# Recurrent stage of a two-layer network: unrolled, and its three engines' operations put in a new order

## The reference, cut to what matters

```python
x = layernorm(x, ln0_w, ln0_b)
for l in range(L):                                   # L = 4
    h = layernorm(x, ln1_w[l], ln1_b[l])
    hh = time_shift(h)                               # the token before
    xk = h * tmk[l] + hh * (1 - tmk[l])              # xv, xr alike
    k = jnp.einsum('btc,oc->bto', xk, Wk[l])         # v alike
    sr = jax.nn.sigmoid(jnp.einsum('btc,oc->bto', xr, Wr[l]))
    rwkv = sr * wkv(time_decay[l], time_first[l], k, v)
    x = x + jnp.einsum('bto,co->btc', rwkv, Wo[l])
    h = layernorm(x, ln2_w[l], ln2_b[l])
    hh = time_shift(h)                               # xk, xr from h, hh
    kf = jnp.square(jax.nn.relu(jnp.einsum('btc,fc->btf', xk, Wck[l])))
    kv = jnp.einsum('btf,cf->btc', kf, Wcv[l])
    x = x + jax.nn.sigmoid(jnp.einsum('btc,oc->bto', xr, Wcr[l])) * kv
```

## Time and profile before

| | us |
|---|---|
| median of 3 runs | 1193.19 (1193.03 to 1208.87) |
| the profiled execution | 1198.58, span 1196.7 |
| recurrent stage in it | 728.0 to 1115.2 |
| busy in the span: TensorE, VectorE, ScalarE | 1063.7, 767.2, 578.4 |

### The profile page before, as it was taken

One profiled execution on the slowest core, in us unless ns is written; L12 is line 12 of the kernel. 1 busy time (PEld: TensorE's weight loads), 2 busy tenths in 40 slices (PEclk: granted clock), 3 DMA queues, 4 the chain that ended last, 5 costly groups with the idle time before them and its releaser, 6 DMA issues. The chain is left out here.

```text
span 1196.7 us, 13244 instructions
## 1 busy us (share of the span) xinstructions
PE 1063.7 (89%) x4046; PEld 463.8 (39%) x4046; DVE 767.2 (64%) x1327; ACT 578.4 (48%) x904; POOL 12.1 (1%) x26
## 2 busy tenths in 40 slices
PE   6788999999779999999999996498898898898698
PEld 3333444444334444444444432133333333343332
DVE  5867788887556555555555554676776776776465
ACT  5224566667644222222222224666666666767332
POOL 1000000000000000000000000000000000000000
PEclk9768999999989999999999999799899899899899
DMA  3721022200141545555555520000000000000100
GB/s 116 207 60 41 11 50 50 51 24 10 30 90 40 123 91 117 125 122 113 114 108 125 125 45 28 0 21 9 1 20 9 0 20 0 0 0 1 27 9 26
DMA packets 49975, 64.62 MB, mean 54 GB/s; under 512 B 17570, under 2 KB 41232, under 8 KB 45328
## 3 DMA queue, kind: packets, MB, share of 16 engines
q1 hardware_dynamic: 49100, 63.28, 22.5%
q10 hardware_dynamic: 832, 0.79, 0.2%
HBM read 55.87 MB, written 5.77 MB: 52 GB/s over the span
## 5 line engine op out<-in xcount | busy, mean ns | idle before, releaser
L1098 DVE TENSOR_REDUCE part_max<-psum 128x1 f32<-128x512 f32 (+3 forms) x304 | 188.1, 659 | 54.0 <-PE psum L709 31.6
L945 ACT ACTIVATE pt<-psum 128x1024 f32<-128x1024 f32 (+1 forms) x192 | 151.1, 813 | 141.1 <-PE psum L729 104.0
L1257 DVE TENSOR_TENSOR moe_gu<-moe_silu,psum 128x512 f32<-128x512 f32 x132 | 90.8, 688 | 152.0 <-PE psum L861 147.2
L1082 ACT ACTIVATE moe_silu<-psum 128x512 f32<-128x512 f32 x112 | 66.9, 597 | 200.0 <-PE psum L856 200.0
L856 PE MATMUL psum<-h,moe_wt 128*128 128x512 f32 x264 | 135.6, 595 | 1.6 <-ACT moe_silu L1050 1.6
L861 PE MATMUL psum<-h,moe_wt 128*128 128x512 f32 x264 | 135.2, 593 | 0.5 <-DVE moe_gu L1257 0.5
L866 PE MATMUL psum<-moe_hid,moe_wt 128*128 128x512 f32 x264 | 135.0, 593 | 0.7 <-DVE moe_hid L1265 0.7
L705 PE MATMUL psum<-ka,qa 72*128 72x512 bf16 (+3 forms) x384 | 121.8, 360 | 5.5 <-DMA ka<-rows_k 3.5
L726 PE MATMUL psum<-qa,ka 75*128 75x512 bf16 (+3 forms) x384 | 107.8, 344 | 7.1 <-DMA qa<-neg_t 6.8
L1265 DVE TENSOR_TENSOR moe_hid<-moe_gu,qa 128x512 f32<-128x512 f32 x120 | 83.1, 693 | 13.6 <-DVE moe_gu L1257 5.7
L1542 PE MATMUL psum<-kf,wt_c 128*128 128x512 f32 x128 | 67.8, 656 | 24.2 <-ACT kf L1671 24.2
(11 more groups left out here) (251 smaller groups left out, 1394.7 us busy)
## 6 DMA issues: line engine op xcount, KB each, us to landing
qa<-comb_rows SPq DMA_DIRECT2D x56, 512.0 KB, 6.2
qa<-rows_q SPq DMA_DIRECT2D x21, 192.0 KB
ka<-rows_k SPq DMA_DIRECT2D x21, 192.0 KB
o_den<-acc SPq DMA_DIRECT2D x32, 64.0 KB, 2.2
moe_raw<-in_L_ffn_eg_w SPq DMA_DIRECT2D x32, 64.0 KB, 5.6
moe_raw<-in_L_ffn_eu_w SPq DMA_DIRECT2D x32, 64.0 KB, 5.4
moe_raw<-in_L_ffn_ed_w SPq DMA_DIRECT2D x32, 64.0 KB, 5.1
qa<-comb_rows SPq DMA_DIRECT2D x16, 128.0 KB, 3.1
```

The costliest lines, as they stand in the source:

```text
L945: act.activation(pt[:, u % 4, :, 0:n], score_bank[u % 2][:, :, 0:n], ACT.Exp, scale=SCALE)\
L1082: act.activation(sg[:, c % 2, :], g_bank[:, :], ACT.Silu).then_inc(silu_done, 1)
L1098: dve.tensor_reduce(part_max[:, h0:h0 + heads, slot], bank_of("fill", f)[:, 0:heads * nk].rearrange("p (h n) -> p h n", h=heads), AX_X, AL ...
L1257: dve.tensor_tensor(gu[:, at % 2, :], sg[:, at % 2, :], u_bank[:, :], ALU.mult).then_inc(gu_done, 1)
```

## The change

All loops over units are unrolled in Python, so each instruction has constant operands and waits. The per-sublayer copies of parameters (`vectors_a`, `vectors_c`, L1727 to L1737) go, and the parameters are read in place. Each helper now issues the work of one chunk, and each engine has a `body(u)` for u = 1 to 8 that lists the single operations. With p = u - 1, it holds the time norm and the keys, values and receptance of u, and the output, the channel norm and the channel products of p. The products `gated` of a unit and the product with the gates, `finish` and `residual` stand at the start of the next body on VectorE. On ScalarE `log_den` and `inverse` stand there too, so the sigmoid is no longer ahead of them. The time weights have two buffers. The weights' transposes are spread over the body. The last body does in place of a time norm the norm of the first two chunks for the final stage. At the stage's start the sigmoid of unit 0 stands ahead of the inverse, and `gate_time` and `finish` behind the entry norm of batch 1.

```diff
+def here(u, q):
+    return hp[:, u % 2, 1 + q * CH:1 + (q + 1) * CH]
+def before(u, q):
+    return hp[:, u % 2, q * CH:(q + 1) * CH]
+def vec(v, u):
+    return G.vec[:, 4 * v + u // 2:4 * v + u // 2 + 1]
-def layers(eng, body):
-    with eng.Fori(0, LAYERS - 1) as l:
-        body(l, 0)
-        body(l, 1)
-    body(LAYERS - 1, 0)
-    body(LAYERS - 1, 1, last=True)
+    return n0 + 4 * u + 8 + q
-    with sp.Fori(0, LAYERS - 1) as l:
+    for l in range(LAYERS - 1):
-def turn_c(l, u):
+def turn_c(l, i):
+    if i < 2 and l:
+        pe.wait_ge(relu_done, 8 * (2 * l - 1) + 7 + i)
+    if i < 2 and not l:
+        pe.wait_ge(v_kept, 1 + i)
+    if i == 2:
+        pe.wait_ge(r_mid, 2 * (2 * l) + 2)
     pe.wait_ge(c_in, 48 * (l + 1))
-    for i in range(9):
-        if i == 8:
-            pe.wait_ge(r_mid, 2 * u + 2)
-        mm = pe.transpose(G.bank[(6, 7, 5)[i // 4]][:, chunk(i % 4, P)], raw_c[:, i, :], G.ident[:, :])
-        if i % 4 == 3 or i == 8:
-            mm.then_inc(c_turned, 1)
...
-def body(l, b, last=False):
-    u = 2 * l + b
-    for q in range(2):
-        pe.wait_ge(r_new, 2 * u + q + 1)
-        if not last:
-            ln_centre(pe, G, ln_time(u + 1, q), G.r[:, seq(1 - b, q)], q)
-        output(u, q)
-        if not last:
-            ln_variance(pe, G, ln_time(u + 1, q), q)
-    if not last:
-        if b == 0:
-            turn_c(l, u)
-        else:
-            turn_a(l + 1)
-    norm(lambda q: ln_channel(u, q), b, lambda q: pe.wait_ge(r_mid, 2 * u + q + 1))
-    if last:
-        for c in range(2):
-            pe.wait_ge(G.x_l1, c + 1)
-            ln_centre(pe, G, G.ln_count + c, G.x[:, chunk(c)])
-        for c in range(2):
-            ln_variance(pe, G, G.ln_count + c)
-    if not last:
-        if b == 0:
-            pe.wait_ge(c_kept, 3 * (l + 1))
-        else:
-            pe.wait_ge(a_kept, l + 2)
-        kvr(u + 1, 1 - b)
-    channel_mix(u, last)
...
+def time_centre(u, q):
+    if u == UNITS:
+        pe.wait_ge(G.x_l1, q + 1)
+        ln_centre(pe, G, ln_time(u, q), G.x[:, chunk(q)], q)
+    else:
+        if u:
+            pe.wait_ge(r_new, 2 * u - 1 + q)
+        ln_centre(pe, G, ln_time(u, q), G.r[:, seq(u % 2, q)], q)
+def keys(u, q):
+    if u == UNITS:
+        return
+    pe.wait_ge(h_time, 2 * u + q + 1)
+    if q == 0:
+        pe.wait_ge(a_kept, u // 2 + 1)
+    if q == 1 and u % 2:
+        pe.wait_ge(c_kept[2], u // 2 + 1)
+    shifted(G.bank[4 + q], u, K_HERE, K_BEFORE, q).then_inc(k_psum, 1)
+def values(u, q):
+    if u == UNITS:
+        return
+    if u % 2:
+        pe.wait_ge(c_kept[q], u // 2 + 1)
+    shifted(G.bank[6 + q], u, V_HERE, V_BEFORE, q).then_inc(v_psum, 1)
+def receptance(u, q):
+    if u == UNITS:
+        return
+    if u:
+        pe.wait_ge(G.ln.scaled, ln_channel(u - 1, q) + 1)
+        shifted(G.bank[q], u, R_HERE, R_BEFORE, q).then_inc(r_psum, 1)
+    else:
+        pe.wait_ge(k_kept, q + 1)
+        shifted(G.bank[4 + q], u, R_HERE, R_BEFORE, q).then_inc(r_psum, 1)
 def output(u, q):
-    pe.wait_ge(wd, STEPS * u + 17 + q)
-    pe.matmul(G.bank[4 + q][:, :], wt_a[:, WO, :], rw[:, chunk(q)], start=True, stop=True).then_inc(o_psum, 1)
...
+def up(u, q, j):
+    n = 4 * q + j
+    if n == 0:
+        pe.wait_ge(c_kept[0], u // 2 + 1)
+    if n < 2 and u < LAST:
+        pe.wait_ge(v_kept, 2 * (u + 1) + n + 1)
+    else:
+        pe.wait_ge(relu_done, 8 * u + n - 1)
+    if j == 0:
+        pe.wait_ge(mixed_k, 2 * u + q + 1)
+    pe.matmul(G.bank[6 + j % 2][:, :], wt_c[:, WCK + j, :], mix_c[:, 0, q, :], start=True, stop=True)\
+        .then_inc(f_psum, 1)
+def down(u, q, j):
+    pe.wait_ge(kf_done, 8 * u + 4 * q + j + 1)
+    if j == 0 and u < LAST:
+        pe.wait_ge(k_kept, 2 * (u + 1) + q + 1)
+    if j == 0 and u == LAST:
+        pe.wait_ge(r_mid, 2 * u + q + 1)
+    if q == 0 and j == 0:
+        pe.wait_ge(c_kept[1], u // 2 + 1)
+    mm = pe.matmul(G.bank[4 + q][:, :], wt_c[:, WCV + j, :], kf[:, j, q, :], start=(j == 0), stop=(j == 3),
+                   skip_group_check=True)
+    if j == 3:
+        mm.then_inc(kv_psum, 1)
+def gate(u, q):
+    if q == 0:
+        pe.wait_ge(c_kept[2], u // 2 + 1)
+    pe.wait_ge(mixed_r, 2 * u + q + 1)
+    pe.wait_ge(G.ln.rstd, ln_channel(u, q) + 1)
+    pe.matmul(G.bank[2 + q][:, :], wt_c[:, WCR, :], mix_c[:, 1, q, :], start=True, stop=True)\
+        .then_inc(cr_psum, 1)
+def body(u):
+    p, l = u - 1, u // 2
+    time_centre(u, 0)
+    if u % 2:
+        turn_c(l, 1)
+    time_variance(u, 0)
+    time_centre(u, 1)
+    output(p, 0)
+    time_variance(u, 1)
+    output(p, 1)
+    channel_centre(p, 0)
+    if u % 2:
+        turn_c(l, 0)
+    channel_variance(p, 0)
+    channel_centre(p, 1)
+    keys(u, 0)
+    if u % 2:
+        turn_c(l, 2)
+    channel_variance(p, 1)
+    keys(u, 1)
+    values(u, 0)
+    values(u, 1)
+    up(p, 0, 0)
+    up(p, 0, 1)
+    up(p, 0, 2)
+    receptance(u, 0)
+    up(p, 0, 3)
+    up(p, 1, 0)
+    down(p, 0, 0)
+    up(p, 1, 1)
+    up(p, 1, 2)
+    gate(p, 0)
+    up(p, 1, 3)
+    receptance(u, 1)
+    gate(p, 1)
+    down(p, 0, 1)
+    down(p, 1, 0)
+    down(p, 0, 2)
+    if u % 2 and u < LAST:
+        turn_a(l + 1)
+    down(p, 1, 1)
+    down(p, 0, 3)
+    down(p, 1, 2)
+    down(p, 1, 3)
...
+def keep_a(l):
+    act.wait_ge(a_turned, l + 1)
+    wt = wt_a[l % 2]
+    for i in range(3):
+        turned = G.bank[6][:, chunk(i, P)]
+        act.activation(wt[:, 2 * i, :], turned, ACT.Copy, scale=vec(TMK + i, 2 * l))
+        act.activation(wt[:, 2 * i + 1, :], turned, ACT.Copy, scale=rest[:, 4 * i + l:4 * i + l + 1])
+    act.copy(wt[:, WO, :], G.bank[6][:, chunk(3, P)]).then_inc(a_kept, 1)
+def log(n, q):
+    act.wait_ge(G.ln.variance, n + 1)
+    if n >= 2:
+        act.wait_ge(G.ln.scaled, n - 1)
+    act.activation(G.rs[:, q, :], G.bank[2 + q][:, :], ACT.Ln, bias=G.eps[:, 0:1]).then_inc(G.ln.logged, 1)
+def rstd(n, q):
+    act.wait_ge(G.ln.logged, n + 1)
+    act.activation(G.rs[:, q, :], G.rs[:, q, :], ACT.Exp, scale=-0.5).then_inc(G.ln.rstd, 1)
...
+def sigmoids(u):
+    if u:
+        act.wait_ge(cr_psum, 2 * u)
+    if u == 0:
+        act.wait_ge(r_psum, 2)
+        act.activation(gates[:, 0:2, :], banks[:, 4:6, :], ACT.Sigmoid).then_inc(sig_done, 1)
+    elif u == UNITS:
         act.activation(gates[:, 2:4, :], banks[:, 2:4, :], ACT.Sigmoid).then_inc(sig_done, 1)
-def body(l, b, last=False):
-    u = 2 * l + b
-    if not last:
-        for q in range(2):
-            ln_square(act, G, ln_time(u + 1, q), q)
-            ln_rstd(act, G, ln_time(u + 1, q), q)
-        if b == 0:
...
+def body(u):
+    p, l = u - 1, u // 2
+    log_den(p, 0)
+    if u % 2 == 0 and u < UNITS:
+        keep_a(l)
+    square(ln_time(u, 0), 0)
+    log_den(p, 1)
+    inverse(p, 0)
+    inverse(p, 1)
+    log(ln_time(u, 0), 0)
+    square(ln_time(u, 1), 1)
+    rstd(ln_time(u, 0), 0)
+    log(ln_time(u, 1), 1)
+    rstd(ln_time(u, 1), 1)
+    square(ln_channel(p, 0), 0)
+    if u % 2:
+        keep_c(l, 0)
+    log(ln_channel(p, 0), 0)
+    rstd(ln_channel(p, 0), 0)
+    square(ln_channel(p, 1), 1)
+    if u % 2:
+        keep_c(l, 2)
+    keep_k(u, 0)
+    log(ln_channel(p, 1), 1)
+    rstd(ln_channel(p, 1), 1)
+    keep_k(u, 1)
+    if u % 2:
+        keep_c(l, 1)
+    keep_v(u, 0)
+    keep_v(u, 1)
+    relu(p, 0, 0)
+    square_relu(p, 0, 0)
+    relu(p, 0, 1)
+    relu(p, 0, 2)
+    decay(u, "e2b", e2b, 1.0)
+    square_relu(p, 0, 1)
+    decay(u, "e1b", e1b, -1.0)
+    relu(p, 0, 3)
+    relu(p, 1, 0)
+    square_relu(p, 0, 2)
+    decay(u, "e1", e1, -1.0)
+    relu(p, 1, 1)
+    decay(u, "e2", e2, 1.0)
+    square_relu(p, 0, 3)
+    relu(p, 1, 2)
+    square_relu(p, 1, 0)
+    square_relu(p, 1, 1)
+    relu(p, 1, 3)
+    square_relu(p, 1, 2)
+    sigmoids(u)
+    square_relu(p, 1, 3)
...
+def time_scale(u, q):
+    if u == UNITS:
+        ln_scale(dve, G, ln_time(u, q), G.h[:, chunk(q)], G.mod[:, 1, 4, 0:1], q)
+    else:
+        ln_scale(dve, G, ln_time(u, q), here(u, q), vec(LN1W, u), q)
...
+def addend(u):
+    if u == UNITS:
+        return
+    dve.wait_ge(v_kept, 2 * u + 2)
+    dve.wait_ge(wkv_act, after_act(u, "e2b"))
+    dve.tensor_tensor(num[:, :], e2b[:, :], v_s[:, :], ALU.mult).then_inc(wkv_dve, 1)
+def scans(u):
+    dve.wait_ge(wkv_act, after_act(u, "e1b"))
+    dve.wait_ge(wkv_dve, after_dve(u, "num"))
+    dve.tensor_tensor_scan(aa[:, 1:S + 1], e1b[:, :], num[:, :], 0.0, ALU.mult, ALU.add).then_inc(wkv_dve, 1)
+    dve.tensor_tensor_scan(bb[:, 1:S + 1], e1b[:, :], e2b[:, :], 0.0, ALU.mult, ALU.add).then_inc(wkv_dve, 1)
+def fractions(u):
+    dve.wait_ge(wkv_act, after_act(u, "e2"))
+    dve.tensor_tensor(n2[:, :], e2[:, :], v_s[:, :], ALU.mult).then_inc(wkv_dve, 1)
+    dve.wait_ge(wkv_dve, after_dve(u, "bb"))
+    dve.tensor_tensor(den[:, :], e1[:, :], bb[:, 0:S], ALU.mult).then_inc(wkv_dve, 1)
+    dve.tensor_tensor(num[:, :], e1[:, :], aa[:, 0:S], ALU.mult).then_inc(wkv_dve, 1)
+    dve.wait_ge(wkv_dve, after_dve(u, "den"))
```

(63 more changed lines are left out.)

431 lines of the change are left out of this document (185 added, 246 removed).

## The result

The changed kernel took 1153.3 us (median of 5 runs, 1148.0 to 1159.2) against 1198.4 us for the kernel before (5 runs, 1193.0 to 1208.9). The ratio is 0.9616, with a 95% interval of 0.9559 to 0.9674: 46 us of 1198, between 39 and 53. In a later session on one chip, with 6 and 11 runs, it was 1148.0 against 1199.7, ratio 0.9574 (0.9536 to 0.9612), which is 51 us (47 to 56). The ratios leave out executions in a slower state with a lower granted clock, one of the 6 and one of the 11, and in the same way elsewhere.

A forecast was written before the change was run, and what follows sets the result against it. The prediction held that no engine was full and waits between the three engines set the unit. Units -46.9, first start +1.5, head -3.5 and tail +3.3 gave -45.6 us: 1148 us from the median 1193.2, range 1131 to 1168.

The forecast's parts named there:

- the wait of 3.43 us for the square: TensorE's down products wait for ScalarE's last square: 24.0 us in six units, then two matmuls take 3.43 instead of 1.72.
- The walk: Predicted timing of one unit in the new order: first `up` at 17.9 us, unit end at 37.2, mean 37.5.
- the ScalarE line that I let set the end: Second part of a unit: ScalarE works without a gap from 19.0 to 36.3 us, last down product done at 37.2.
- my signs of being wrong: VectorE waits for exponentials ahead of scans, gated products wait for `down`, or granted clock drops in a unit's first part.
- the first rival: A wait is left in every unit, one late exponential delaying VectorE's scans: 41 us a unit, 1169 us; chance 0.15.
- rival 4: More gain than forecast, hand-offs hidden as well: 36.0 us a unit, -60.9 instead of -46.9, 1134 us; chance 0.12.
- The allowance of 0.5 us for hand-offs: Added to each unit's mean of 37.5 us for hand-offs rounded away, giving 38.0.
- this term: The seven units: from 312.9 us to 266 at 38.0 each, -46.9, plus 1.5 for the first start; -45.4 us.
- the slow start of the first unit: The first of the seven units starts at 1.2 GHz after TensorE idled 11.81 us: +1.5 us.
- The tail: Stage end, after the last down products to the last add: 30.2 us before, 33.5 after; +3.3, between 0 and +6.
- The head: Stage start: the entry norm of batch 1 goes first and centring starts sooner; -3.5 us, between 0 and -5.
- The rival with half clock in the first part of each unit: TensorE at 1.2 GHz for all 14 matmuls up to the second keys: 12.0 us a unit, 1232 us; chance 0.04.

The follow-up runs named there:

- Experiment 1: The kernel before with its one loop over sublayers written out in Python, nothing else; mean step 44.37 us against 44.61, one execution 1215.1 us.
- experiment 2: The kernel before with the last two relus and squares put ahead of the sigmoid on ScalarE; mean step 42.70 us, ratio to before 0.9940.
- experiment 3: The changed kernel with the inverse of the denominator put back ahead of the last square on ScalarE; 1165.1 us, ratio to before 0.976, mean step 38.72.
- experiment 5: The changed kernel with the four receptance matmuls put back ahead of all up products; mean step 40.07 us, execution 1169.8 us.
- experiment 4: The changed kernel with the channel norm's two chunks together again on TensorE and in ScalarE's queue; mean step 37.57 us, +0.60.
- Experiment 6: The changed kernel with one more 128x512 matmul (0.86 us) on TensorE in each of seven units; mean step 37.83 us, up 0.85.
- 7: The changed kernel with one more activation (0.95 us) on ScalarE ahead of the sigmoid in each of seven units; mean step 37.63 us, up 0.65.
- Experiment 8: The changed kernel with one more product (1.13 us) on VectorE ahead of the denominator in each of seven units; mean step 37.21 us, up 0.24.

## Why the prediction came out, and the steps of it that were off

*That the order is the gain, through waits and clock: shown.* The seven units took 53.3 us less with equal work. Experiment 1 puts the unrolling at 0.2 of 7.6 us a unit. How much of the 7.6 is waits and how much clock was not separated by an experiment; two steps of before at full clock put the clock at about 1.5.

*How the stall goes.* I named the wait of 3.43 us for the square first, and said that TensorE pays again behind it; that held in four of seven units. It goes, but experiment 2 shows that removing it alone brings 1.9 us. Put back singly in the changed kernel, the late square costs 1.75 (experiment 3), the early receptance 3.09 (experiment 5), the norm's pairing 0.60 at most (experiment 4). These sum to 5.4 of 7.6 us and need not be independent. Which parts of the order make up the rest was not tried.

*The count of matmuls failed.* I wrote 38 in a unit, in the words on the kernel before as well; it is 40. Norms take 8, output 2, keys, values and receptance 12, up 8, gate 2, down 8, and 7 x 40 x 2 passes with 36 + 12 transposes are the 608 passes of the long windows. TensorE's own work is therefore 40 x 0.86 = 34.4, and 35.8 with the 13 transposes of an odd unit (0.11 each: four start at 886.84 and the next matmul at 887.28), 35.1 in the mean, not 33 to 34. The walk gave the first part 18 matmuls, which is right, and the second 20 where it has 22.

*So the wrong engine bounded the second part of the unit in the prediction.* TensorE alone, which was to be done at 35.1, should have been at 36.8, and 37.4 with the 0.6 taken for transposes; the ScalarE line that I let set the end came to 37.2. The two agree by accident. Experiment 6 against 7 shows which it is: 0.85 of 0.86 us against 0.65 of 0.95, though ScalarE's line is within 0.1 us of it in every second unit. One of my signs of being wrong did appear: the gated products wait for `down`, 0.97 us at 889.27. It says the same, that the down products are what comes last. Experiment 8 corrects VectorE's slack from 0.2 to 0.9 us, so the first rival, a late exponential that delays VectorE, had less for it than I wrote. With the right count TensorE's work alone sets a bound of 35.1 in the mean and not 34, and rival 4's 36.0 us would have left it 0.9 us of waits. It has 1.9 (36.98 - 35.1), where the norms stand. The first part of the walk, with 1.1 us of waits, was right: 17.9 to the first `up`, measured 17.75 in an odd unit and 17.6 in an even one.

*The allowance of 0.5 us for hand-offs was not needed.* The walk without it said 37.2 to 37.5; measured 36.98. Seven times 38.0 instead of 36.98 is 7.1 us of the 7.9 by which this term was too small. The rest is the slow start of the first unit: its centrings did run at a granted clock of 0.50 (778.7 to 780.8), but the seven units are only 0.7 us longer than seven steps, where I had 1.5.

*The tail was mis-sized*: +6.3 for +3.3. The walk put the first centring at 2.5 us, the first `up` at 15.6 and the end at 33.5; measured 2.5, 19.0 (1057.25) and 36.5. So the 3 us lie between the first centring and the first `up`. The walk had TensorE at its full rate there. After 2.37 us of idle its first matmul of two passes takes 1.76 us where 1.12 is usual, with a granted clock of 0.72 up to 1045.0, so the level of 1.2 GHz has a part in them. TensorE also waits 0.69, 0.69, 1.06 and 1.30 us there, and no run tells the two apart. The head was right in kind and size (-4.2 for -3.5).

*The clock*: forecast 0.98 or more, measured 0.99. The rival with half clock in the first part of each unit did not happen: that part has waits of 0.25 us in odd units and 0.69 in even ones, and a granted clock of 1.00 in both units shown (853.5 to 862.6 and 816.9 to 826.0). The rule on short idles between groups of matmuls, from the Trainium skill, "TensorE: Matmul & The Clock Gate", section on the second failure mode, is not borne out by the short waits of this order. Longer ones are another matter, and their length alone does not decide: behind 3.42 us the clock fell in four of seven units of before and in all seven of experiment 1, behind 2.35 to 2.44 in three of six of experiment 2, behind 2.37 at the tail, and behind the 1.82 of experiment 3 it did not.

In all the stage gained 51.2 us in the traces for a forecast of 45.6. The units were 7.9 us better than forecast, the head 0.7 better and the tail 3.0 worse, so misses of opposite sign cancel in part, and that the first timed comparison gave 46 us is partly luck. That comparison (46 us, 39 to 53) holds both; the second (51 us, 47 to 56) holds the traces' value and leaves the forecast just outside.
